# GpSimd adds the product halves of 25 listed couples instead of 17, with twelve product slots and sums eleven groups behind

## The reference

```
e = stack(tbl_f[ids[:, f]] for f in 0..39)                     # 512 x 40 x 64
z[:, p] = sum over e of (v_i @ W_p) * v_j                      # 780 pairs p = (i, j), i < j
h = concat([z, dense_ctx])                                     # 512 x 796
h = relu(h @ W_top1 + b_top1);  h = relu(h @ W_top2 + b_top2)  # 512, then 256 wide
y = h @ W_top3                                                 # 512 x 1
```

## Time and profile before

| | |
|---|---|
| three runs | 349.15, 349.21 and 350.26 us, median 349.21 |
| the profiled execution | 349.04 us, of which the span of the core is 346.9 |
| TensorE matmuls | busy 329.1 us, 95% of the span |
| VectorE | busy 249.6 us, 72% |
| GpSimd | busy 225.6 us, 65%: 144 indirect DMAs (137.8 us) and 37 adds (86.8 us) |
| ScalarE | busy 22.1 us, 6% |
| granted TensorE clock, mean | 0.995 of full speed |

### The profile page before, as it was taken

One profiled execution on the slowest core, in us unless ns is written; L12 is line 12 of the kernel. 1 busy time (PEld: TensorE's weight loads), 2 busy tenths in 40 slices (PEclk: granted clock), 3 DMA queues, 4 the chain that ended last, 5 costly groups with the idle time before them and its releaser, 6 DMA issues.

```text
span 346.9 us, 4306 instructions
## 1 busy us (share of the span) xinstructions
PE 329.1 (95%) x1676; PEld 115.1 (33%) x1676; DVE 249.6 (72%) x248; ACT 22.1 (6%) x35; POOL 225.6 (65%) x191
## 2 busy tenths in 40 slices
PE   0799979899999999999999999999999999999997
PEld 0133333233333333333333333333333333333442
DVE  2484968778787888978889888988888898840000
ACT  1001100000000000000001000010000000000032
POOL 6777777777778889877788788576887423520000
PEclk9999989999999999999999999999999999999999
DMA  6984443243423238731322323232110000000000
GB/s 167 255 231 146 119 106 105 81 102 91 115 57 104 64 96 261 170 104 33 96 85 62 89 68 86 62 69 85 39 23 2 0 3 0 0 2 0 0 2 0
DMA packets 17854, 27.59 MB, mean 80 GB/s; under 512 B 4901, under 2 KB 5029, under 8 KB 17834
## 3 DMA queue, kind: packets, MB, share of 16 engines
q1 hardware_dynamic: 9770, 17.86, 17.7%
q0 software_dynamic: 4608, 4.73, 6.9%
q10 hardware_dynamic: 3456, 4.72, 4.8%
HBM read 22.57 MB, written 0.00 MB: 65 GB/s over the span
## 4 chain that ended last, share of the span: by engine, by line
PE 80%; POOL 13%; issue 4%; DMA 1%; ACT 0%
PE ps_t L421 47%; PE ps_z L443 21%; POOL rows L265 13%; PE ps_t L465 5%; PE ps_e L404 2%; PE ps_t L488 2%; PE ps_e L465 2%; DMA rows<-in_tbl,ids_sb 1%; DMA ids_sb<-in_ids_t 1%; PE ps_t L494 1%; ACT y_sb L328 0%
## 5 line engine op out<-in xcount | busy, mean ns | idle before, releaser
L372 DVE TENSOR_TENSOR prod<-ps_t,E 128x1024 f32<-128x1024 f32 x200 | 231.7, 1217 | 45.7 <-PE ps_t L421 44.9
L421 PE MATMUL ps_t<-E,w_sb 64*128 64x512 f32 x800 | 189.8, 609 | 0.8 <-ACT E L294 0.7
L265 POOL DMA_INDIRECT rows<-in_tbl,ids_sb x144 | 137.8, 957 | 43.4 <-issue 41.9
L272 POOL TENSOR_TENSOR prod<-prod 128x1024 f32<-128x1024 f32 x37 | 86.8, 2370 | 37.4 <-DVE prod L372 37.3
L421 PEld LDWEIGHTS ps_t<-E,w_sb 64*128 64x128 f32 x800 | 71.1, 187 | 109.6 <-issue 82.2
L443 PE MATMUL ps_z<-prod,quads 128*32 128x512 f32 x572 | 76.8, 600 | 0.0
L443 PEld LDWEIGHTS ps_z<-prod,quads 128*32 128x32 f32 x572 | 15.1, 109 | 48.9 <-DVE prod L372 29.1
L351 DVE TENSOR_SCALAR prod<-prod,first_row_f 125x512 f32<-125x512 int32 x38 | 16.6, 495 | 11.1 <-PE ps_e L395 5.1
L294 ACT ACTIVATE E<-ps_e 128x512 f32<-128x512 f32 x18 | 10.8, 598 | 192.4 <-PE ps_e L404 171.1
L395 PE MATMUL ps_e<-prod 125*64 125x512 f32 x40 | 12.1, 694 | 11.2 <-DVE prod L351 10.0
L465 PE MATMUL ps_t<-z,w_sb 128*128 128x512 f32 (+1 forms) x42 | 18.6, 595 | 0.0
(11 more groups left out here) (26 smaller groups left out, 21.1 us busy)
## 6 DMA issues: line engine op xcount, KB each, us to landing
w_sb<-in_w_units SPq DMA_DIRECT2D x50, 256.0 KB, 2.9
E<-E ACTq DMA_DIRECT2D x72, 64.0 KB, 2.3
rows<-in_tbl,ids_sb POOLq DMA_INDIRECT x144, 2.6
w_sb<-in_w SPq DMA_DIRECT2D x7, 256.0 KB, 4.5
prod<-in_ids_by_field SPq DMA_DIRECT2D x2, 512.0 KB, 9.0
prod<-in_tbl SPq DMA_DIRECT2D x3, 312.5 KB
w_sb<-in_w SPq DMA_DIRECT2D x1, 512.0 KB, 7.1
prod<-in_tbl SPq DMA_DIRECT2D x1, 250.0 KB
```

The lines of the kernel that those rows point to most:

```text
L265: pool.indirect_dma_start(rows[:, g % G_RING, b, f * DIM:(f + 1) * DIM], None, tables[2 * k + f], bass.IndirectOffsetOnAxis(ap=ids_sb[:, c ...
L272: pool.tensor_tensor(prod[:, n % P_RING, 0, :, :], prod[:, n % P_RING, 0, :, :], prod[:, n % P_RING, 1, :, :], ALU.add).then_inc(halves_ad ...
L372: dve.tensor_tensor(prod[:, n % P_RING, s, :, :], ps_t[:, (2 * n + s) % STEPS, :, :], multiplier, ALU.mult).then_inc(product_ready, 1)
L421: last = pe.matmul(ps_t[:, step % STEPS, j, :], w_sb[at:at + DIM, m % W_RING, col:col + P], E[at:at + DIM, slot_of(pairs_of(n)[s][j]), :], ...
```

## The change

GpSimd adds in 25 couples that a tuple lists, both groups of each, instead of in every other couple from group 20 on. Of the old list, 17 couples were added in both groups and three (17, 31 and 49) in one group; no couple of the new list has only one. The product ring grows from 8 to 12 slots, the sums run 11 groups behind the products instead of 7, and the weight ring shrinks from 12 to 8. `E4` loses a part that no group reads. The end is written in another order, because six couples instead of four are left to be summed when the last group's products have been issued.

```
-W_RING = 12
-P_RING = 8
+W_RING = 8
+P_RING = 12
 STEPS = 3
-LAG = 7
+LAG = 11
...
-ADDED = [n for n, (_, M) in enumerate(GROUPS) if M is not None and n >= 20 and n // 2 % 2 == 1]
+ADDED_COUPLES = (6, 8, 10, 11, 14, 18, 20, 21, 25, 27, 28, 29, 32, 33, 34, 37, 38, 41, 42, 43, 44, 45, 46, 47, 48)
+ADDED = [n for n in range(NG) if n // 2 in ADDED_COUPLES]
...
-        E4 = sb("E4", [P, QUADS, 2, BATCH])
+        E4 = sb("E4", [P, QUADS - 1, 2, BATCH])
...
-            reduce_two(NG - 6)
             pe.wait_ge(params_loaded, 16 * (CHUNKS + 5))
             pe.wait_ge(z_copied, CHUNKS - 2)
             pe.wait_ge(e_copied, KP)
             sum_h1(0, 0, CHUNKS - 2)
+            for n in range(NG - LAG + 1, NG - 4, 2):
+                reduce_two(n)
+            pe.wait_ge(product_ready, 2 * NG - 2)
+            sum_h1(1, 0, CHUNKS - 2)
+            sum_h1(2, 0, CHUNKS - 2)
             reduce_two(NG - 4)
-            sum_h1(0, CHUNKS - 2, CHUNKS - 1)
-            pe.wait_ge(product_ready, 2 * NG - 2)
-            sum_h1(1, 0, CHUNKS - 1)
             reduce_two(NG - 2)
-            for m in range(2, H1 // P):
-                sum_h1(m, 0, CHUNKS - 1)
+            sum_h1(3, 0, CHUNKS - 2)
+            for m in range(H1 // P):
+                sum_h1(m, CHUNKS - 2, CHUNKS - 1)
```

More of the change, by code:

```diff
@@ L300, in copy_fields @@
                         to, of = (2 * (k % 2) + f) * HALF, f * DIM + h * HALF
-                        act.dma_start(E4[to:to + HALF, k // 2, h, :], E[of:of + HALF, slot_of(k), :]).then_inc(
+                        act.dma_start(E4[to:to + HALF, k // 2 - 1, h, :], E[of:of + HALF, slot_of(k), :]).then_inc(
                             e4_placed[u], 16)
@@ L365, in multiply @@
                     if M is not None:
-                        multiplier = E4[:, M, s, None, :].to_broadcast([P, 2, BATCH])
+                        multiplier = E4[:, M - 1, s, None, :].to_broadcast([P, 2, BATCH])
                     elif s == 0:
```

## The result

The changed kernel is slower: 353.92 us (352.1 to 354.92) against 349.63, a ratio of 1.0115 with a 95% interval of 1.0083 to 1.0147. The prediction said 349.9, about no change, with a range from 347.9 to 351.8. Its profiled execution took 354.92 us, of which the span is 352.7; that is 5.88 more than the profiled execution of before. When the changed kernel was timed again, further down, one of its four executions took 668.14 us, and the ratio given there leaves it out.

The account below looks back on a forecast made before the run. TensorE alone was taken to bound the kernel from 65.76 us on, after GpSimd's gathers. A 2.2 us wait at arrival 12 less 1.46 gained behind it gave +0.74 on 349.04: 349.8, median 349.9, range 347.9 to 351.8.

Parts of the forecast that it names:

- The adds: On TensorE, 25 added couples instead of 17 save 6.88 us; behind arrival 12 the net gain is 1.46 us.
- The lag: Sums of couples 0 and 1 move from a wait to behind arrival 7's transposes, adding 3.70 us to the chain.
- A clock that falls behind arrival 7: After a longer TensorE wait before arrival 7, 3.4 us at half speed: a loss of 1.7 us (bounds 0 and 3.4).
- Arrival 7's time: TensorE starts arrival 7's transposes at 65.8 as before, after 4 us or more of waiting.
- GpSimd's issue: With eight adds ahead of them, GpSimd starts the last of arrival 12's gathers at 131.7, against 117.86 before.
- TensorE's arrival there: TensorE comes to arrival 12's transposes at 133.7: 133.71, less 1.72 us for added couples, plus 1.7 for the clock.
- The landing: Arrival 12's last gather lands in 4.2 us beside the parameter loads (bounds 2.4 and 4.7), so TensorE waits 2.2 us.
- The second fall of the clock: Slower rival: the clock falls again behind arrival 12's wait, losing 1.7 us, total 351.5; chance 0.30.
- Costed at nothing: Weight ring of 8, twelve product slots with a lag of eleven, and 13 more GpSimd adds beside VectorE: no cost.

Follow-up runs that it names:

- the run of the lag alone: The changed kernel with the old list of adds, keeping lag 11, twelve product slots, weight ring of 8 and the new end: 355.33 us, ratio 1.015.
- the run with two couples elsewhere: The changed kernel with couples 26 and 30 in the list in place of 10 and 11, still 25 couples: 348.22 us, ratio 0.9965.

## Why the prediction was wrong, point by point

- **The adds** (predicted 8 x 0.86 = 6.88 us, of which 1.46 net are left behind arrival 12): right as far as the traces show it. From arrival 12's transposes to the end of the span were 346.9 - 133.71 = 213.2 us before and are 349.5 - 138.01 = 211.5 with the clock held: 1.7 less.
- **The lag** (3.70 us behind arrival 7): right in size by the run of the lag alone. 6.2 less the clock's 2.6 leaves 3.6, and its execution without that fall has 3.5.
- **A clock that falls behind arrival 7** (1.7 taken): in the changed kernel it fell one arrival sooner, after 2.07 us of waiting before arrival 6 (0.50 at 59 to 60), in time that was to be waited anyway; so the wait before arrival 7 shrank to 1.78 and the clock held there. Where it did fall behind arrival 7, it cost 2.6, not 1.7.
- **Arrival 7's time** (65.8, after 4 us or more of waiting, was a sign of being right; another time a sign of being wrong): it was 66.68. The gathers were late already (arrival 7's last one starts at 64.20 instead of 63.35), by an amount that also differs between executions of one kernel.
- **GpSimd's issue** (last gather of arrival 12 at 131.7): right; 132.57, and 0.84 of the difference were there at arrival 9 already (84.17 against 83.33).
- **TensorE's arrival there** (133.7): 138.64 - 5.72 = 132.92. It is near by two misses that partly cancel: arrival 7 came 0.92 later, and the 1.7 of the clock were not lost (133.71 - 1.72 + 0.92 = 132.91).
- **The landing** (4.2 us, bounds 2.4 and 4.7): the first step that failed, in the words "I take 4.2, between these two (bounds 2.4 and 4.7)". It took 6.02, and 5.2 to 6.73 in the other runs with the loads beside it. The forecast had the loads start at 131.2, half a us ahead of the gather. They started at 130.41, because TensorE did not lose the 1.7 of the clock, and the gather came 0.87 late, so it was issued 2.2 us behind their start (132.57 against 130.41), deeper among them. The upper bound was a gather issued 1.2 us behind it. Those rows were still rising (2.7, 3.7, 4.7), and the bound should have gone on with them. The wait was 5.72 instead of 2.2.
- **The second fall of the clock** (a rival, 0.30, priced at 1.7; nothing in the sum): the second step that failed. It came and cost 7.02 - 4.36 = 2.66. The forecast's own wait of 2.2 was past the 1.43 up to which its rows had the clock hold, so the price belonged in the sum; the fall after 2.07 us before arrival 6 bears that out.
- **Costed at nothing** (the rings, the adds beside VectorE): right. Among TensorE's waits after, none is for a load of W or for an add, and VectorE's steps kept their length (1218 ns in the mean, 1217 before).

Together: arrival 12 starts 138.64 - 133.71 = 4.93 us later, the clock costs 2.66, and 1.7 are gained behind it: 5.9, against 5.88 between the two profiled executions. Against the forecast for such an execution (349.8), the 354.92 us are 5.1 too long: 0.87 for the later gather, 1.82 for the landing and 2.66 for the clock, less 0.24 that were gained in addition behind arrival 12. The mechanism up to the wait and its place were as forecast. The landing was sized too small, and the price of the clock, the largest of the three, stood in a rival although the wait that brings it was part of the forecast itself.

The Trainium skill (DMA: Bandwidth & Descriptors, Issuing engines are not separate DMA queues) has all issuers' transfers interleave on the same engines; the trace agrees more strongly than predicted, with 6.02 us beside 371 GB/s of other loads, and 348.55 us in place of 353.92 when these loads move (the fall of the clock behind the wait goes with them).
The Trainium skill (TensorE: Matmul & The Clock Gate, Why this matters for your kernels) has a pause between bursts of matmuls put the clock back to half rate; the trace agrees, with 0.50 behind the 5.72 us of waiting. Its advice is for longer pauses than some that were enough here (2.07 and 2.15 us); there the measurement decides.

## What to carry to other kernels

An engine that both computes and issues DMAs in program order has free time only where nothing that it issues later is awaited; count each add as a delay of every gather behind it, up to the one that the busy engine waits for. Where a delay lands a small transfer behind large ones, price its landing by the queue it falls into and let the bound go on rising with it. And a wait of the busy engine has a second price, the clock behind it, which belongs in the sum together with the wait, not in a rival beside it.

## What the runs showed of the hardware

- A gather of 128 rows took 2.4 to 2.7 us to land just ahead of the 2.3 MB of parameter loads (the kernel before), and at most 3.3 where they had been moved away. Issued at the start of these loads it took 3.7 us, 1.2 us behind it 4.7, 1.7 to 2.2 us behind it 5.2 to 6.1 (four profiles), and 3.6 us behind it 6.73 (132.55 against 128.96).
- Of TensorE's waits for rows in these profiles, those of 1.78 us and less left the clock at 1.00 and those of 2.07 us and more were followed by 0.50. The length of one wait alone does not settle it: in the run with two couples elsewhere a wait of 1.61 us for VectorE, before the products at 43.07, was followed by 0.50 from 45 to 48 too. One such fall with nothing behind to hide it cost 2.6 to 2.7 us, and matmuls whose result is thrown away, in the wait, kept it from falling.
- 50 adds on GpSimd beside VectorE left VectorE's steps as they were: 1218 ns in the mean after, 1217 before.
